# One pre-norm transformer layer on one core: projections in two runs of four, weighing in one, and divides and token normalisation on GpSimd

## The reference

```
x   = x + attention(layernorm(x))
x   = x + (silu(n @ w_gate.T) * (n @ w_up.T)) @ w_down.T      # n = layernorm(x)

attention(n):
    q, k, v = split(n @ w_attn + b_attn)                        # 32 heads of 16
    scores  = q k^T / 16 + slope[h] * (key - query), causal
    return (softmax(scores) @ v) @ w_proj + b_proj
```

## Time and profile before

| | |
|---|---|
| median of 3 runs | 922.75 us (920.37 to 922.88) |
| the profiled execution: own time | 921.12 us |
| its span | 919.4 us |
| PE, DVE, ACT, POOL busy in the span | 860.3, 477.3, 364.1, 183.5 us |

### The profile page before, as it was taken

How to read it: one execution, slowest core, us unless ns; L and a number is a source line. 1 busy time by engine, 2 the same in 40 slices (tenths; PEclk the granted TensorE clock), 3 DMA queues, 4 the chain that set the end, 5 groups by cost and what they waited for, 6 DMA issues and landing times. The chain is left out here.

```text
span 919.4 us, 13759 instructions
## 1 busy us (share of the span) xinstructions
PE 860.3 (94%) x5088; PEld 580.1 (63%) x5088; DVE 477.3 (52%) x931; ACT 364.1 (40%) x693; POOL 183.5 (20%) x337
## 2 busy tenths in 40 slices
PE   1999799999999999999998579999999999999998
PEld 1755355556555565555543268887888788878886
DVE  6586577766777667776773154443222322232223
ACT  4345455565556655565555233322111211111111
POOL 4223233342433324333342300000000000000000
PEclk9999899999999999999999879999999999999999
DMA  8764445655565455735461364203000310021001
GB/s 267 207 208 140 122 146 170 185 155 161 177 207 164 137 171 186 227 112 170 143 207 49 113 227 155 89 0 137 2 1 1 96 41 0 0 77 60 0 0 46
DMA packets 70562, 109.33 MB, mean 119 GB/s; under 512 B 13395, under 2 KB 38662, under 8 KB 70505
## 3 DMA queue, kind: packets, MB, share of 16 engines
q1 hardware_dynamic: 68457, 108.32, 37.5%
q10 hardware_dynamic: 2048, 0.27, 0.2%
HBM read 65.97 MB, written 42.32 MB: 118 GB/s over the span
## 5 line engine op out<-in xcount | busy, mean ns | idle before, releaser
L839 DVE TENSOR_REDUCE bm<-bank 128x3 f32<-128x384 f32 (+1 forms) x384 | 223.0, 596 | 118.8 <-PE bank L1045 114.7
L700 ACT ACTIVATE pt<-bank 128x512 f32<-128x512 f32 (+1 forms) x384 | 196.8, 528 | 168.4 <-PE bank L1067 162.9
L1067 PE MATMUL bank<-q_st,k_st 116*128 116x512 bf16 (+3 forms) x512 | 136.7, 309 | 18.0 <-DMA q_st<-mt 10.5
L1336 DVE TENSOR_TENSOR gu<-bank,silu 128x512 f32<-128x512 f32 x44 | 30.5, 692 | 220.2 <-issue 132.7
L1147 PE MATMUL bank<-fT_hi,wgu_hi 128*128 128x512 f32 x352 | 138.8, 394 | 5.5 <-DVE wgu_lo L1308 3.5
L1043 PE MATMUL bank<-k_st,q_st 97*128 97x512 bf16 (+3 forms) x512 | 141.6, 302 | 0.8 <-DMA q_st<-slopes_dram 0.6
L1147 PE MATMUL bank<-fT_lo,wgu_hi 128*128 128x512 f32 x352 | 138.4, 393 | 0.0
L1147 PE MATMUL bank<-fT_hi,wgu_lo 128*128 128x512 f32 x352 | 137.7, 391 | 0.0
L1067 PEld LDWEIGHTS bank<-q_st,k_st 116*128 116x128 bf16 x512 | 41.7, 98 | 131.0 <-ACT pt L700 72.1
L1045 PE MATMUL bank<-mask_qk,identb 128*128 128x128 bf16 x512 | 106.4, 220 | 0.0
L610 POOL TENSOR_SCALAR_AFFINE_SELECT pt<-pt 128x256 f32<-128x256 f32 x128 | 52.7, 412 | 213.1 <-ACT pt L700 213.1
(11 more groups left out here) (95 smaller groups left out, 1217.0 us busy)
## 6 DMA issues: line engine op xcount, KB each, us to landing
stack_dram<-part SPq DMA_DIRECT2D x32, 384.0 KB, 2.6
q_st<-stack_dram SPq DMA_DIRECT2D x32, 384.0 KB
k_st<-stack_dram SPq DMA_DIRECT2D x32, 384.0 KB
stack_dram<-part SPq DMA_DIRECT2D x32, 256.0 KB, 3.1
pv_dram<-weighed SPq DMA_DIRECT2D x32, 256.0 KB, 4.8
weighed<-pv_dram SPq DMA_DIRECT2D x17, 256.0 KB
xt<-x SPq DMA_DIRECT2D x16, 256.0 KB, 4.3
stack_dram<-part SPq DMA_DIRECT2D x32, 128.0 KB, 3.9
```

The costliest lines, as they stand in the source:

```text
L700: act.activation(pt[:, h % PT_RING, COL0[k]:COL0[k] + WIDE[k]], bank[3 + (3 * h + k) % 2][:, 0:WIDE[k]], ACT.Exp, scale=1.0 / HD).then_inc ...
L839: dve.tensor_reduce(bm[:, h % 4, BM_AT[k]:BM_AT[k] + BM_N[k]], bank[k][:, 0:BM_N[k] * P].rearrange("p (n q) -> p n q", q=P), AX.X, ALU.max ...
L1067: last = pe.matmul(bank[3 + u % 2][:, at:at + n], k_st[0:K_EXP, s, h % 4, t * P:(t + 1) * P], q_st[0:K_EXP, s, h % 4, t * P:S], start=True ...
L1336: dve.tensor_tensor(gu[:, f % 2, :], bank[5 + 2 * (f % 2)][:, :], silu[:, f % 2, :], ALU.mult).then_inc(gu_done, 1)
```

## The change

- PE: a head's 8 projection products come in two runs of four, each right behind `shifted_scores` of parts 0 and 1 and ahead of `scores`. `weigh_values` is one run after part 1 of head 0. `transpose_maxima` moves to the first part of head 1. In `shifted_scores` the two tiles of part 1 change order (the same columns of the bank).
- ScalarE: `copy_pv` after the third exponential of head 0; `place_maxima` at the end of head 1.
- VectorE: `copy_maxima` in head 1 behind `scored(1)`; the divides of all groups but the last and the token normalisation leave it.
- GpSimd: a divide stands ahead of the head's `clear_future` (behind `third_part` in head 3), a token tile is normalised behind it.

```diff
@@ -618,6 +618,16 @@
                 pool.wait_ge(xr_in[t % 2], 16 * (2 * b + t // 2 + 1))
                 pool.tensor_tensor(xr(b, t), xr(b, t), bproj[:, :], ALU.add).then_inc(xr_biased, 1)
 
+            def normalise_tokens(b, t):
+                pool.wait_ge(rstd_ready, b + 1)
+                pool.tensor_scalar(xt[:, t, :], xt[:, t, :], mv[:, t, 0:1], rstd[:, t:t + 1], ALU.subtract,
+                                   ALU.mult).then_inc(normed, 1)
+
+            def divide(a, i):
+                at = slice(i * HS, (i + 1) * HS)
+                pool.wait_ge(attn_in, (a + 1) * 32)
+                pool.tensor_tensor(attnT[:, at], attnT[:, at], sums[:, at], ALU.mult).then_inc(attn_ready, 1)
+
             reciprocal_deviation(0)
             for k in range(2):
                 pool.wait_ge(w_hi_done, k + 1)
@@ -637,7 +647,11 @@
                         for kind, mb, g in made(c)[:1]:
                             if kind == "Q":
                                 third_part(kind, mb, g)
+                    if divides(c, i) is not None:
+                        divide(*divides(c, i))
                     clear_future(4 * c + i)
+                    if normalised_at(c) is not None:
+                        normalise_tokens(normalised_at(c), i)
                     if i == 0:
                         for kind, mb, g in made(c - 1)[1:]:
                             if kind == "K":
@@ -751,8 +765,6 @@
                     exponential(h, 0)
                     if tokens_at(c, i) is not None and i == 0:
                         transposed_hi(*tokens_at(c, i))
-                    if i == 1 and c > 0:
-                        copy_pv(c - 1)
                     if i == 3:
                         for tile in made(c)[:1]:
                             if tile[0] == "Q":
@@ -763,13 +775,15 @@
                     if highs(c, i) is not None:
                         attention_hi(*highs(c, i))
                     exponential(h, 2)
+                    if i == 0 and c > 0:
+                        copy_pv(c - 1)
+                    if i == 1 and c + 1 < CHUNKS:
+                        place_maxima(c + 1)
                     if i == 0:
                         for tile in made(c - 1)[1:]:
                             if tile[0] == "K":
                                 second_part(*tile)
                     if i == 2:
-                        if c + 1 < CHUNKS:
-                            place_maxima(c + 1)
                         for tile in made(c)[:1]:
                             read_tile(*tile)
             attention_hi(*highs(CHUNKS, 0))
@@ -857,9 +871,8 @@
                 dve.wait_ge(attn_in, GROUPS * 32)
                 return dve.reciprocal(sums[:, q * P:(q + 1) * P], sums[:, q * P:(q + 1) * P])
 
-            def divide(a, i):
+            def divide_last(i):
                 at = slice(i * HS, (i + 1) * HS)
-                dve.wait_ge(attn_in, (a + 1) * 32)
                 dve.tensor_tensor(attnT[:, at], attnT[:, at], sums[:, at], ALU.mult).then_inc(attn_ready, 1)
 
             def attention_lo(a, i):
@@ -881,12 +894,6 @@
                 if t == TT - 1:
                     step(last)
                     moments(dve, stats, mv, moments_ready)
-
-            def normalise_tokens(b, t):
-                dve.wait_ge(moments_ready, b + 1)
-                dve.wait_ge(rstd_ready, b + 1)
-                dve.tensor_scalar(xt[:, t, :], xt[:, t, :], mv[:, t, 0:1], rstd[:, t:t + 1], ALU.subtract,
-                                  ALU.mult).then_inc(normed, 1)
 
             for k in range(KT):
                 transposed_lo(0, k)
@@ -918,21 +925,17 @@
                             block_maxima(ahead, k)
 
                     scored(0)
-                    if i == 2 and c + 1 < CHUNKS:
-                        copy_maxima(c + 1)
                     if i == 3:
                         for tile in made(c)[:1]:
                             read_tile(*tile)
                     scored(1)
+                    if i == 1 and c + 1 < CHUNKS:
+                        copy_maxima(c + 1)
                     if i == 0:
                         for tile in made(c - 1)[1:]:
                             if (tile[0], tile[2]) != ("P", 3):
                                 read_tile(*tile)
-                    if divides(c, i) is not None and not (late(c) and i == 2):
-                        divide(*divides(c, i))
                     scored(2)
-                    if late(c) and i == 2 and divides(c, i) is not None:
-                        divide(*divides(c, i))
                     if i == 1:
                         for kind, b, t in made(c - 1)[1:]:
                             if (kind, t) == ("P", 3):
@@ -948,19 +951,17 @@
                     if statistics_at(c) is not None:
                         for t in ((0,), (1, 2), (3,), ())[i]:
                             token_statistics(statistics_at(c), t)
-                    if normalised_at(c) is not None:
-                        normalise_tokens(normalised_at(c), i)
 
             for i in range(HALVES):
                 for a, half in lows(CHUNKS, i):
                     attention_lo(a, half)
             invert_sums(0)
             step(invert_sums(1))
-            divide(LAST, 0)
+            divide_last(0)
             invert_sums(2)
             attention_lo(LAST, 0)
             step(invert_sums(3))
-            divide(LAST, 1)
+            divide_last(1)
             attention_lo(LAST, 1)
             for t in range(TT):
                 add_projection(B - 1, t)
@@ -1061,12 +1062,11 @@
                     pe.wait_ge(m_placed[c % 2], (c // 2 + 1) * 32)
                 u = 3 * h + k
                 need(pe, exp_done, u - 1)
-                at = 0
-                for t in T_TILES[k]:
+                for t in T_TILES[k][::-1]:
                     n = S - t * P
+                    at = S - P if t == 3 else 0
                     last = pe.matmul(bank[3 + u % 2][:, at:at + n], k_st[0:K_EXP, s, h % 4, t * P:(t + 1) * P],
                                      q_st[0:K_EXP, s, h % 4, t * P:S], start=True, stop=True)
-                    at += n
                 last.then_inc(t_done, 1)
 
             def weigh_values(c, tiles):
@@ -1112,18 +1112,15 @@
                         transpose_tokens(*tokens_at(c, 0))
                     for k in range(3):
                         shifted_scores(h, k)
+                        if i > 0 and k < 2:
+                            between(c, 8 * (i - 1) + 4 * k, 8 * (i - 1) + 4 * k + 4)
                         scores(h + AHEAD, k)
-                        if i > 0:
-                            between(c, 8 * (i - 1) + 3 * k, 8 * (i - 1) + min(3 * k + 3, 8))
-                        if i == 0 and c > 0:
-                            if k == 1:
-                                weigh_values(c - 1, (0,))
-                            if k == 2:
-                                weigh_values(c - 1, (1, 3, 2))
+                        if (i, k) == (0, 1) and c > 0:
+                            weigh_values(c - 1, (0, 1, 3, 2))
+                        if (i, k) == (1, 0) and c + 1 < CHUNKS:
+                            transpose_maxima(c + 1)
                         if (i, k) == (1, 0) and tokens_at(c, 1) is not None:
                             transpose_tokens(*tokens_at(c, 1))
-                    if i == 1 and c + 1 < CHUNKS:
-                        transpose_maxima(c + 1)
             weigh_values(CHUNKS - 1, (0, 1, 3, 2))
             for k in range(2, KT):
                 for t in range(TT):
```

## The result

The kernel is not faster: 923.43 us (median of 20 runs, 921.34 to 930.33) against 921.47 (20 runs, 917.89 to 926.01), ratio 1.0029 with an interval of 1.0016 to 1.0043. The forecast was 914.5. The profiled execution took 921.34 (span 919.6), against 921.12 (span 919.4) for the one of before: the pair that can be compared row by row differs by 0.2 only. It is the fastest of the changed kernel's twenty runs, so its trace shows a lucky execution; where that matters, the other traces are named.

A forecast was written before the change was run, and what follows sets the result against it. The order of work on PE (TensorE), busy 94% of the span, was taken to bound the kernel. Savings of -22.7 and costs of +14.4 gave -8.3: 912.8 us profiled, 914.5 on the median's scale, range 906 to 926.

The forecast's parts named there:

- the Q chain: Head 3 of Q chunks: maxima, remainder, cast, second exponential and next score come 0.92 later; +6.8 us over twelve heads.
- moves that cost nothing: Moving copy_pv behind head 0's third exponential and issuing the placing earlier (1.15 of ScalarE, covered by four products): 0.
- the weighing's full -6.7: Weighing the values in one run instead of two saves 0.23 in each of 29 chunks: -6.7 us.
- the normalisation on GpSimd: Batch 1's tokens normalised in chunk 1, 0.75 for the last piece, so chunk 2's transposes start later: +1.5 us.
- The entries: Projection runs start behind a wide shifted score instead of a short mask product: 0.17 a head, 65 heads, -11.1 us.
- rival (b): Runs cost as much behind a wide product, as PE might not load fp32 weights early: about 925 us; chance 0.12.
- The extra 0.5 for attention_hi: In chunks 4, 12 and 20 attention_hi stands ahead of the third exponential, next score 0.16 late: +0.5 us.
- Rival (a): The Q remainder starts as early as before, so all 78 heads gain: -21.4, 901 us; chance 0.10.
- The late weighing: In six Q chunks a GpSimd divide ahead of the select makes the weighing wait some 0.6: +3.6 us.
- rival (c): PE's new idle gaps drop the granted clock to 0.50, up to 2.7 each; 933 to 950 us; chance 0.07.
- -2.9: Maxima placed one head earlier shorten chunk 3's wait by 1.5 and halve the 2.7 slow stretch behind it: -2.9 us.
- The last stretch: In chunk 31 GpSimd's divides stand ahead of the selects, so the last weighing starts later: +2.0 us.

The follow-up runs named there:

- a_rem: The changed kernel with VectorE taking Q's remainder ahead of the first block maxima in head 3 of Q chunks; 913.87 us, 0.9915 of the kernel before.
- a_rem_dve: The changed kernel with Q's remainder first and the divides and token normalisation back on VectorE; 907.46 us, 0.985 of the kernel before.
- best1: a_rem_dve with VectorE reading head 0's token tile ahead of the third maxima; 907.82 us, 0.9848 of the kernel before.
- b_weigh: The kernel before with the values weighed in one run after the second part of head 0; 919.6 us, 0.9979.
- b_runs: The kernel before with projection products in runs of four behind shifted scores and the reversed tile order; 925.22 us, 1.0032.
- best2: best1 with the maxima transposed, copied and placed at their old places; 913.59 us, 0.9881 of the kernel before.
- a_last: The changed kernel with the divides of head 3 and of the last chunk behind GpSimd's selects; 919.11 us, 0.9989 of the kernel before.
- a_dve: The changed kernel with the group divides and token normalisation back on VectorE at their old places; 915.29 us, 0.9929 of the kernel before.

## Why the prediction was wrong

The direction was forecast wrong: 914.5 with 0.74 for faster, and a ratio of 1.0029 came, above 1 and just inside the bound of 0.3% that I had called the same (0.14). The time itself, 923.4, lies inside the range of 906 to 926.

The step that failed is the list of what becomes late. The gains on PE and the price of the Q chain came as forecast, but the products that move back on PE were taken to cost nothing outside that chain ("moves that cost nothing", the weighing's full -6.7), and the normalisation on GpSimd was put at 0.75 us. The runs showed 4.2 us for token tiles that VectorE reads late and 2.07 us for each normalisation, which with the clock behind it made chunk 1 dearer by 2.7 than forecast; two smaller terms are below.

Right by the head lengths:
- The entries. 0.17 a head in head 1 and 0.2 in heads 2 and 3, 0.23 for one weighing run less, so the rows from chunk 31 did hold in the steady part; rival (b) is out.
- The Q chain: 4.36 forecast, 4.27 (nine) and 4.36 (three) measured, 51.5 together against 45.6, +5.9 where I had +6.8. The extra 0.5 for attention_hi (L730) came one head later, in head 0 of chunks 5, 13 and 21, 3.90 instead of 3.73: the third exponential stands behind it and ends at 127.78, and the second shifted score waits for that, 0.58 behind the first where it is 0.50 in chunk 9. In a_rem, a_rem_dve and best1 these heads are 3.73 or 3.74. Chunk 5 in the changed kernel:

```profile
127.01 0.50 ACT L730 ACTIVATE aT_hi<-weighed,bias_qkv 128x256 fp32r<-128x256 f32 x1
127.26 0.38 PE L1068 MATMUL bank<-q_st,k_st 116*128 116x512 bf16 x1 [0.91 <-ACT pt L714]
127.41 0.37 ACT L714 ACTIVATE pt<-bank 128x256 f32<-128x256 f32 x1
...
127.84 0.39 PE L1068 MATMUL bank<-q_st,k_st 116*128 116x128 bf16 x2
```

  Rival (a) did not come about, yet a_rem shows that its mechanism was one reordering away.
- The late weighing: +3.7 in six chunks against +3.6.
- The clock stayed up behind the Q gaps of 0.9 to 1.2 (1.00 on average from 236 to 498 us); in this trace rival (c) holds for chunk 1 alone.

Failed, by size:
- **"Moves that cost nothing" and the weighing's -6.7.** Both looked at PE's own products and not at who comes later on the other engines. Token tiles late in their banks: +1.8 in head 1 of chunks 2 and 3, +0.8 in head 1 and +1.4 in head 2 of chunks 10, 18 and 26, +0.2 in 11, 19 and 27, 4.2 together. The head 1 part is b_weigh's; that of head 2 (in chunk 10 VectorE's fT_lo ends at 210.10 and L1004, which fills the same bank, starts at 210.20 after a wait of 0.22; the rest is not traced) is not in b_weigh and only 0.1 a head in b_runs. It is not in best2 either (3.31, 3.29 and 3.31), which has both parts, but in best1 (3.68), which differs from it by the early maxima alone: it comes from the runs of four and the early maxima together.
- **The normalisation in chunk 1**, +1.5 forecast (up to +5 with the half clock, and the half clock came), +4.2 over head 3 and the next head, by a 2.07 that I had put at 0.75 from the select, which has one input and no scalars read per partition, and by the half clock. My range ended at 1.33, from the addition; the true price lay outside what any row of before bounded. The Trainium skill (GPSIMD Engine Reference, 4.1) calls one-input work on GpSimd roughly line-rate; the trace disagrees for this form, which reads one tile and two scalars of each partition: 2.07 us against VectorE's median of 0.54 for the same tile, nearly four times. For the divide, two inputs, the trace comes near the page's about two (0.734 against 0.422, 1.7).
- **The placing's 1.15 of issue** was covered by four products, but chunks 2, 3, 28 and 29 have no products to project. +2.0 in head 2 of chunks 2 and 3, and the like in 28 and 29 (there given back in head 3). In this trace the waits removed were larger than forecast (-2.9 was less than half of the 6.7 that head 3 of chunk 3 and head 0 of chunk 4 gave back, 0.2 of it by the weighing), so the maxima's net is -6.2 against -4.9. That is luck: in the seven other kernels with early maxima the same two heads give back 1.3 to 6.0, in the median 3.4. So the -2.9 was about right, and the surplus in this execution hides a part of the loss.
- **Head 0 of chunks 12, 20 and 28** has +2.4 together that I did not see: VectorE, in order, stands in the projection's addition (L843) until GpSimd's bias addition is done, which starts when its tokens land, and PE's scores wait for the maxima behind it. Chunk 12 in the changed kernel:

```profile
229.73 1.26 POOL L619 TENSOR_TENSOR xr<-xr,bproj 128x512 f32<-128x512 f32 x1 [2.52 <-DMA xr<-x]
...
231.10 0.69 DVE L843 TENSOR_TENSOR xr<-bank,xr 128x512 f32<-128x512 f32 x1 [2.33 <-POOL xr L619]
...
232.31 0.34 PE L1044 MATMUL bank<-k_st,q_st 97*128 97x384 bf16 x1 [0.79 <-DVE bm L853]
```

- **The last stretch** +3.1 instead of +2.0. The change's own rows are the three of the end above. In the traces, without divides on GpSimd kernels end in 405.4 to 409.0, with them, a_last aside, in 410.4 to 411.4.

Ledger against the forecast -8.3: tokens +4.2, chunk 1 +2.7, head 0 of 12, 20 and 28 +2.4, head 0 of 6 and 22 at 3.90 and 4.03 +0.5 (not traced further), end +1.1, start +0.6, Q chain -0.9, maxima -1.3: +9.3, where the profiles differ from it by +8.5.

Open: the profile pair gives +0.2, the medians +2.0 (ratio: +2.7). The times of one kernel spread over 8 to 9 us, and each trace is one draw, in which the late landings fall otherwise. The wait ahead of chunk 4 is one that varies: with its median over the seven other early kernels the profiled execution would have been 3.3 us longer, which would more than fill the gap between +0.2 and +2.0 (an estimate; other waits vary too). Every other kernel profiled started chunk 0 at 56.0 to 57.9 against 55.8, though none touches that part: 0.2 to 2 us of it may be the luck of that one profile of before.

## What to carry over

When a run on the bottleneck engine is merged, list for each product that moves back every reader on the other engines, follow each in its fixed order to the next product that waits for it, and move the head of the longest chain forward: here the remainder ahead of the maxima turned a loss of 0.3% into a gain of 0.9%. Idle time of an engine is no cover by itself; what counts is whether the moved instruction stands ahead of one that PE waits for, which is why the divides ahead of the selects cost 0.57 in each of the late heads, and nearly nothing behind them. And check each "covered by" in the chunks that lack the cover.

## What the runs showed of the hardware

- A normalisation (subtract and multiply by two scalars of each partition, 128x512 fp32) took 2.07 to 2.35 us on GpSimd and 0.45 to 0.54 for most on VectorE; an elementwise product of 128x256 0.73 and 0.42.
- The granted clock fell behind PE waits of 4.34 (0.57 over the 4 us behind it) and 4.38, and, in a_rem, 3.47 (0.50 over 3 us). The fall cost 1.6, 2.7 and 2.6 us in the head behind it (5.35, 6.66 and 6.30). The length of the wait alone does not tell whether it falls: behind 2.57 (b_runs, 0.59 over 4 us) and 1.88 (a_rem_dve, 0.60) it fell, behind 2.56 (a_dve) and 1.88 (best1) it stayed at 1.00.
- Two DMAs of a few KB issued by ScalarE kept it from 95.32 to 96.82 from its next exponential, and such DMAs took 1.6 to 7.6 us to land (6.3 at most before, 7.6 in best1). What made the slow ones slow was not tested.
